# A graph layer's message sums: half-unit padding ahead of odd blocks, and in the last stage selectors on GpSimd, a floor in PSUM, and turning between the sums

## The chip, the cores and the metric

The kernel runs on one core of a Trainium2 chip. The metric is the device time of one execution in microseconds, the median of several runs. The engines are TensorE (PE in the profile, its weight loads PEld), VectorE (DVE), ScalarE (ACT), GpSimd (POOL) and SyncE (SP), which here only issues DMAs.

## The reference

```python
x, src, dst, edge = ...        # (6250, 128), (100000,), (100000,), (100000, 128), float32
h = concatenate([x[src], x[dst], edge]) @ W + b
h = (h - mean(h)) * rsqrt(var(h) + 1e-5) * gamma + beta
msg = relu(h)
out = segment_sum(msg, src, 6250)
return layernorm(x + out)
```

`src` and `dst` are drawn at random; the edges are sorted by `dst`. The sum goes over `src`, which is unsorted.

## The kernel before

Nodes are cut into `NB` = 49 blocks of 128 by `src`, edges into `NG` = 98 groups of 1024 in the order given. The work has three parts.

**Groups.** For each group the edge features are turned and multiplied by the last third of W, the `dst` part is added by a one-hot matmul, and the 1024 rows of 129 numbers (128 values and the node's number in its block) are scattered by GpSimd, eight indirect DMAs a group (L677), to a DRAM buffer `rows`, sorted by the block of `src`. Each block has a region there: its edges in order of arrival, and behind them `UNIT` = 256 rows of padding, whose node number is -1, so that it meets no selector. The start of each region is made from the block counts at the beginning (`room_of`, `end_at`, `start`). SP writes the padding (`fill_pad`, L531), four blocks per group in the first 13 groups, from one SBUF tile `fill`; the last block's padding goes first, since idle places of the list read it.

**Pairs.** The filled regions are read back in units of 256 rows, two units (a pair) at a time. A list made on the chip (`list_rows`, `list_places`, `list_entries`) gives each place the block and the offset of its unit, in the order in which units become full. Four places are given to each group from group 7 on; where too few units are full, a place stays idle and reads padding. A pair `s` goes through these steps, spread over several steps of the loop so that the engines work on different pairs at once:

- SP loads its 512 rows to `hs` (`load_pair`, four steps ahead, when the buffer is free after `pre`, L546).
- VectorE compares node numbers with `iota_row`: `sel`, 128x512, one-hot (`selectors`, L1582), two steps ahead. The four buffers come free with the sums.
- TensorE turns `sel` (`turn_selectors`, L924, one step ahead), ScalarE copies it to `selT` (`copy_selT`, L1169), TensorE picks the `src` part of each row, twelve matmuls (`select_a`, L934).
- VectorE adds the loaded rows to it: `pre` (`add_pair`, L1557). ScalarE sums squares (L1177) and takes the root (L1183), VectorE the reciprocal (L1565).
- VectorE scales and applies the floor, which stands for beta and relu: four operations, 128x128 each (`messages`, L1573), with `floor` in SBUF.
- TensorE sums the messages into blocks with `sel` (`sum_tile`, L910, four tiles of two matmuls), two steps later, and VectorE adds both results to `sums` (`add_run`, L1549), three steps later.

Steps 0 to 173 are written into the groups' loop, two per group. From 174 on they run alone: this is the drain (`drain_trips`), written out to step 179 and then as a loop of trips of four steps, whose number is computed on the chip from the number of full units and idle places (`trips`). `TRIP_ADD` is -304 and the shift 3. In the drain each engine runs its own list in order:

```python
PE:   turn_selectors(s+1); sum_pair(s-2); select_a(s+1)
ACT:  copy_selT(s+1); squares(s); roots(s)
DVE:  add_pair(s); add_run(s-3, 0); root_inverse(s-1); add_run(s-3, 1); messages(s-1); selectors(s+2)
```

The order between engines is by semaphores alone: turning waits for `n_sel`, selecting for ScalarE's copy (`n_selTc`), `pre` for `n_a`, sums for `n_msg`, selectors for `n_o` (the sums that used their buffer) and for the loaded rows. GpSimd has no work in the drain.

**Final rows.** y = sums times gain (GpSimd, L709), plus x and more terms, then the layer norm (VectorE L1775 to L1792, ScalarE) and the output.

## Time and profile before

| | us |
|---|---|
| median of 3 runs | 1763.23 (1761.63 to 1763.72) |
| profiled execution | 1767.91 |
| its span on the core | 1766.0 |
| VectorE, TensorE, ScalarE, GpSimd busy | 960.2, 1214.0, 718.9, 770.3 |

The profile is of one execution. Its page gives the busy time of each engine over the whole span and in slices; the trace behind it can be asked for any stretch. Times in the rows count from the start of the span. The groups end near 1585 us, the drain near 1723.

### The profile page before, as it was taken

The numbers are of one execution on the slowest core, as the hardware profiler recorded it, in microseconds if no ns is written. First come the engines' busy times: TensorE is split into PE (matmuls) and PEld (weight loads), VectorE is DVE, ScalarE is ACT, GpSimd is POOL, SyncE is SP. The second block draws the span as 40 slices with busy tenths as digits, with TensorE's granted clock in tenths as the row PEclk, the third lists the DMA queues.
The fourth block names the chain that finished last, engine by engine and source line by source line (L and its number), as shares of the span: only waits on it lengthen the run. The fifth ranks groups of instructions, "written<-read, shape, count | busy, mean of one in ns | idle before, by whom it ended". The sixth has DMA issues, their size and how long they took to land.

```text
span 1766.0 us, 36601 instructions
## 1 busy us (share of the span) xinstructions
PE 1214.0 (69%) x10009; PEld 1061.0 (60%) x10010; DVE 960.2 (54%) x2822; ACT 718.9 (41%) x2854; POOL 770.3 (44%) x808
## 2 busy tenths in 40 slices
PE   6688766676676766666666666766666766647775
PEld 5555656666566665666666566665656666546662
DVE  7633345555455555445545545554455545439997
ACT  4223333434334443334434434443334433336766
POOL 0334555444454445455444455444555444550003
PEclk9778788778778878788887888787788778869998
DMA  7544444444434444444444444444344434313322
GB/s 213 165 116 130 134 145 146 128 113 120 138 116 129 129 117 116 123 130 130 123 115 122 130 122 129 127 112 131 112 130 128 127 111 119 108 57 91 90 67 73
DMA packets 184266, 214.69 MB, mean 122 GB/s; under 512 B 51478, under 2 KB 133610, under 8 KB 184080
## 3 DMA queue, kind: packets, MB, share of 16 engines
q1 hardware_dynamic: 158044, 159.86, 33.8%
q0 software_dynamic: 25088, 51.83, 8.4%
q8 instruction: 83, 1.36, 0.3%
q10 hardware_dynamic: 948, 0.79, 0.2%
q14 instruction: 103, 0.84, 0.2%
HBM read 145.91 MB, written 66.47 MB: 120 GB/s over the span
## 4 chain that ended last, share of the span: by engine, by line
PE 41%; another core or an unknown queue 22%; issue 18%; ACT 9%; DVE 6%; DMA 2%; DVEq 2%; SPq 0%; ACTq 0%
PE bank L956 11%; PE bank L934 7%; PE bank L910 7%; PE bank L850 5%; ACT late L1177 4%; PE bank L924 3%; PE bank L963 2%; DVE late L1573 2%; ACT turn L1139 2%; PE bank L840 1%; PE bank L838 1%; DVEq L490 1%; DMA tabB<-room 1%; ACT late L1183 1%
## 5 line engine op out<-in xcount | busy, mean ns | idle before, releaser
L677 POOL DMA_INDIRECT rows<-p,pos_idx x784 | 754.3, 962 | 825.4 <-ACT p L1143 537.3
L1139 ACT COPY turn<-bank 128x512 f32<-128x512 f32 x196 | 114.8, 586 | 705.1 <-remote 533.1
L956 PE MATMUL bank<-wc,turn 128*128 128x128 f32 x1552 | 300.8, 354 | 67.4 <-ACT turn L1139 54.7
L934 PE MATMUL bank<-room 128*128 x2640 | 251.8, 250 | 93.7 <-issue 67.2
L956 PEld LDWEIGHTS bank<-wc,turn 128*128 128x128 f32 x1552 | 260.5, 254 | 92.2 <-ACT turn L1139 77.5
L934 PEld LDWEIGHTS bank<-room 128*128 128x128 bf16 x2640 | 208.7, 115 | 115.1 <-issue 104.0
L1177 ACT ACTIVATE late<-room 128x128 f32<-128x128 f32 x880 | 260.7, 302 | 3.0 <-issue 1.5
L1573 DVE SCALAR_TENSOR_TENSOR late<-room,late,floor 128x128 f32<-128x128 f32 x880 | 252.6, 349 | 0.8 <-issue 0.5
L910 PE MATMUL bank<-late 128*128 128x129 f32 x1504 | 233.3, 299 | 25.9 <-issue 23.5
L910 PEld LDWEIGHTS bank<-late 128*128 128x128 f32 x1504 | 211.8, 215 | 18.6 <-issue 18.2
L1169 ACT COPY room<-bank 128x512 bf16<-128x512 bf16 x220 | 129.2, 587 | 210.6 <-remote 111.1
L1557 DVE TENSOR_TENSOR room<-bank,room 128x512 f32<-128x512 f32 x132 | 90.7, 687 | 190.0 <-remote 189.4
L850 PE MATMUL bank<-ident,p 128*128 128x128 f32 x784 | 147.7, 320 | 37.8 <-issue 36.5
L1557 DVE TENSOR_TENSOR room<-bank,late 128x512 f32<-128x512 f32 x88 | 60.4, 687 | 204.1 <-remote 204.0
L1177 ACT ACTIVATION_READ_ACCUMULATOR late<-room 128x1 f32 x880 | 168.2, 191 | 0.0
L840 PE MATMUL bank<-turn,before 128*128 128x50 bf16 x704 | 58.2, 202 | 151.3 <-issue 151.3
L840 PEld LDWEIGHTS bank<-turn,before 128*128 128x128 bf16 x704 | 44.0, 113 | 182.6 <-issue 182.6
L850 PEld LDWEIGHTS bank<-ident,p 128*128 128x128 f32 x784 | 102.1, 167 | 63.4 <-issue 62.8
L1549 DVE TENSOR_TENSOR room<-room,bank 128x129 f32 x440 | 126.2, 287 | 23.6 <-issue 19.3
L924 PE MATMUL bank<-ident_bf,late 128*128 128x128 bf16 x752 | 86.1, 243 | 46.0 <-DVE late L1582 28.6
L1143 ACT COPY p<-bank 128x512 f32<-128x512 f32 x196 | 111.7, 570 | 6.2 <-PE bank L963 3.2
L963 PE MATMUL bank<-win,turn 126*128 126x128 bf16 x784 | 97.6, 261 | 0.0
(237 smaller groups left out, 1255.4 us busy)
## 6 DMA issues: line engine op xcount, KB each, us to landing
p<-in_edge_attr_dram SPq DMA_DIRECT2D x98, 512.0 KB
room<-rows SPq DMA_DIRECT2D x264, 129.0 KB
near_bc<-near SPq DMA_DIRECT2D x98, 256.0 KB
late<-rows SPq DMA_DIRECT2D x176, 129.0 KB
rows<-p,pos_idx POOLq DMA_INDIRECT x784
rows<-fill SPq DMA_DIRECT2D x49, 129.0 KB, 3.2
win<-tabB SPq DMA_DIRECT2D x196, 31.5 KB
tabB<-room SPq DMA_DIRECT2D x12, 384.0 KB, 3.2
```

Source lines behind the costliest of these rows:

```text
L677: nc.gpsimd.indirect_dma_start(rows_ap, bass.IndirectOffsetOnAxis(pos_idx[:, k, j:j + 1], 0), stage[:, k, j, :], None).then_inc(st_free[k] ...
L850: mm = pe.transpose(bank[E_BANK][:, t * P:(t + 1) * P], e_sb[:, k, j * D:(j + 1) * D], ident[:])
L910: mm = pe.matmul(o[:, jj // UJ, :], sel[kk][:, jj, :], msg_room[:, o_at(s, c, -2), jj, :], start=(jj % UJ == 0), stop=(jj % UJ == UJ - 1))
L924: mm = pe.transpose(turned[:, j * P:(j + 1) * P], sel_top[sel_at(s, c, 1, fused)][:, j, :], ident_bf[:])
L934: mm = pe.matmul(bank[A_BANK + b2][:, jj * D:(jj + 1) * D], selT[b2][:, jj * P:(jj + 1) * P], tabA[:, bass.ds(at[jj // UJ], 1), part, :], ...
L956: pe.matmul(bank[H_BANK + h][:, t * D:(t + 1) * D], eT[h][:, t * P:(t + 1) * P], wc[:, 2, :], start=(t == 0), stop=False, skip_group_check ...
L963: mm = pe.matmul(bank[H_BANK + h][:, t * D:(t + 1) * D], pick_t, win[0:WR, k, h, :], start=False, stop=(t == 3), skip_group_check=True)
L1139: nc.scalar.copy(eT[h], bank[E_BANK][:]).then_inc(eT_ready, 1)
L1169: nc.scalar.copy(selT[b2], turned).then_inc(n_selTc, 1)
L1177: a = nc.scalar.activation(junk[b2][:, j, :], pre[b2][:, j, :], ACT.Square, accum_out=ssq[:, b2, j:j + 1])
L1557: nc.vector.tensor_tensor(pre[b2], bank[A_BANK + b2][:].rearrange("p (j d) -> p j d", j=SJ), hs[kk][:, :, 0:D], ALU.add).then_inc(n_pre, 1)
L1573: a = nc.vector.scalar_tensor_tensor(msg_room[:, b2, j, 0:D], pre[b2][:, j, :], rstd[:, b2, j:j + 1], floor[:], ALU.mult, ALU.max)
```

## The change

Four things are changed.

1. Each odd block's region begins with `SHIFT` = 128 rows of padding. `front` holds 0 for even blocks and 128 for odd ones; `base` is the region's start and `start` that of its edges. The list counts units from `base`. The padding of an even block is written together with the next block's front: 384 rows in one DMA. The source tile `fill` is now one row of 129 numbers per partition, repeated, so each DMA's pieces are 516 bytes instead of 1032. Even blocks are written first, and the first load of a pair waits for all 25 of them.
2. In the drain, from step `BY_POOL` = 178 on, GpSimd makes the selectors, with four operations of 128x128 instead of one of 128x512.
3. The floor is copied to PSUM once, in step 177, and the messages from step 178 on read it there.
4. In the drain TensorE turns the selectors of the next pair between the second and the third of the four sum tiles, no longer ahead of them.

```diff
+    SHIFT = UNIT // 2
+        BY_POOL = FUSED + 4
             def fill_pad(bk):
-                at = sp.value_load(pad_i[0:1, bk:bk + 1], min_val=0, max_val=E + NB * UNIT)
-                sp.dma_start(rows_ap[bass.ds(at, UNIT), :].rearrange("(p j) c -> p (j c)", j=UJ),
-                             fill_rows).then_inc(s_fill0 if bk == NB - 1 else s_fill, 16)
+                n = UNIT + SHIFT if bk % 2 == 0 and bk < NB - 1 else UNIT
+                at = sp.value_load(pad_i[0:1, bk:bk + 1], min_val=0, max_val=E + NB * UNIT + NB // 2 * SHIFT)
+                sp.dma_start(rows_ap[bass.ds(at, n), :].rearrange("(p j) c -> p j c", j=n // P),
+                             fill[:].to_broadcast([P, n // P, ROW])).then_inc(s_fill if bk % 2 else s_fill0, 16)
+
+            pads = [bk for bk in range(NB) if bk % 2 == 0] + [bk for bk in range(NB) if bk % 2]
+            EVEN = (NB + 1) // 2
...
-                    if isinstance(g, int) and 1 <= g and 4 * g - 4 < NB - 1:
-                        for bk in range(4 * g - 4, min(4 * g, NB - 1)):
+                    if g >= 1:
+                        for bk in pads[4 * g - 4:4 * g]:
                             fill_pad(bk)
...
                         if s + FETCH == 0:
                             sp.wait_ge(s_list, 1)
-                            sp.wait_ge(s_fill0, 16)
+                            sp.wait_ge(s_fill0, 16 * EVEN)
...
+            nc.gpsimd.memset(front[:, 0:BK:2], 0.0).then_inc(s_iota, 1)
+            nc.gpsimd.memset(front[:, 1:BK:2], float(SHIFT)).then_inc(s_iota, 1)
...
+            def selectors(s, c, q, r):
+                hk = hs_at(s, c, q, r, 2)
+                pool.wait_ge(hs_ready[hk[0]], hk[1] * 32)
+                pool.wait_ge(n_o, s - 1)
+                settle()
+                for j in range(SJ):
+                    a = nc.gpsimd.tensor_scalar(sel[(c + 2) % RING][:, j, :], iota_row[:], hs[hk[0]][:, j, D:ROW], None, ALU.is_equal)
+                a.then_inc(n_sel, 1)
+
+            def step(s, c, q, r, on):
+                if isinstance(s, int) and s < BY_POOL:
+                    return
+                if isinstance(s, int) and s == BY_POOL:
+                    pool.wait_ge(n_sel, BY_POOL + 2)
+                if on(2):
+                    selectors(s, c, q, r)
+            drain_trips(pool, trip_count(pool), step)
...
             def step(s, c, q, r, on):
                 if on(1):
                     at = entry(pe, regs, blk_i, s + 1, NB - 1)
-                    turn_selectors(s, c)
-                if on(-2):
-                    sum_pair(s, c)
+                for jj in range(SJ):
+                    if jj == SJ // 2 and on(1):
+                        turn_selectors(s, c)
+                    if on(-2):
+                        sum_tile(s, c, jj)
                 if on(1):
                     select_a(s, c, at)
...
-            link(nc.vector.tensor_scalar(room_of[:], bank[3][:, 0:BK], float(UNIT), None, ALU.add))
+            link(nc.vector.scalar_tensor_tensor(room_of[:], bank[3][:, 0:BK], float(UNIT), front[:], ALU.add, ALU.add))
             link(nc.vector.tensor_tensor_scan(end_at[:], room_of[:], room_of[:], 0.0, ALU.add, ALU.bypass))
-            nc.vector.tensor_tensor(start[:], end_at[:], room_of[:], ALU.subtract).then_inc(s_base, 1)
+            link(nc.vector.tensor_tensor(base[:], end_at[:], room_of[:], ALU.subtract))
+            nc.vector.tensor_tensor(start[:], base[:], front[:], ALU.add).then_inc(s_base, 1)
...
-                nc.vector.tensor_copy(fl_i[:, 0, :], cum[:])
-                link(nc.vector.tensor_tensor(fl_i[:, 1, :], cum[:], cnt[:], ALU.subtract))
+                link(nc.vector.tensor_tensor(fl_i[:, 0, :], cum[:], front[0:NR, :], ALU.add))
+                link(nc.vector.tensor_tensor(cum[:], cum[:], cnt[:], ALU.subtract))
+                link(nc.vector.tensor_tensor(fl_i[:, 1, :], cum[:], front[0:NR, :], ALU.add))
...
                 if on(-1):
-                    messages(s, c)
-                if on(2):
+                    messages(s, c, floor[:] if isinstance(s, int) and s < BY_POOL else floor_ps)
+                if on(2) and isinstance(s, int) and s < BY_POOL:
                     selectors(s, c, q, r, iota_row[:])
+                if isinstance(s, int) and s == BY_POOL - 1:
+                    dve.wait_ge(st_ready, 2 * NG)
+                    nc.vector.tensor_copy(floor_ps, floor[:]).then_inc(s_floor_ps, 1)
+                    dve.wait_ge(s_floor_ps, 1)
```

## Rows read from the trace of the kernel before

**Rows 1.** The page's busy times by engine, and its group of all messages.

```profile
PE 1214.0 (69%) x10009; PEld 1061.0 (60%) x10010; DVE 960.2 (54%) x2822; ACT 718.9 (41%) x2854; POOL 770.3 (44%) x808
...
L1573 DVE SCALAR_TENSOR_TENSOR late<-room,late,floor 128x128 f32<-128x128 f32 x880 | 252.6, 349 | 0.8 <-issue 0.5
```

**Rows 2.** Stretches: length, busy PE, PEld, DVE, ACT, POOL, clock, DMA share, GB/s.

```profile
500.00:1000.00 500.00, 341.77 (x2912) 310.19 (x2911) 260.24 (x745) 197.39 (x812) 246.15 (x256) 0.81 0.44 124
...
1640.00:1680.00 40.00, 31.09 (x338) 27.43 (x338) 39.23 (x126) 28.79 (x140) 0.00 (x0) 1.00 0.33 93
```

**Rows 3.** Groups by line, 1600 to 1708 us: busy us, mean ns, idle us.

```profile
L1582 DVE TENSOR_TENSOR late<-iota_row,room 128x512 f32<-128x512 f32 x38 | 26.0, 685 | 0.0
L1557 DVE TENSOR_TENSOR room<-bank,room 128x512 f32<-128x512 f32 x37 | 25.4, 686 | 0.0
L1169 ACT COPY room<-bank 128x512 bf16<-128x512 bf16 x37 | 21.7, 586 | 29.8 <-PE bank L924 29.8
...
L924 PE MATMUL bank<-ident_bf,late 128*128 128x128 bf16 x148 | 14.4, 219 | 24.4 <-DVE late L1582 24.4
```

**Rows 4.** Timeline of one drain step: start us, length us, engine, line.

```profile
1656.49 0.69 DVE L1557 TENSOR_TENSOR room<-bank,room 128x512 f32<-128x512 f32 x1
...
1656.71 0.38 PE L924 MATMUL bank<-ident_bf,late 128*128 128x128 bf16 x4 [0.53 <-DVE late L1582]
...
1656.93 1.11 PE L910 MATMUL bank<-late 128*128 128x129 f32 x8
...
1657.13 0.59 ACT L1169 COPY room<-bank 128x512 bf16<-128x512 bf16 x1 [0.67 <-PE bank L924]
...
1657.71 1.14 DVE L1573 SCALAR_TENSOR_TENSOR late<-room,late,floor 128x128 f32<-128x128 f32 x4
...
1657.88 1.03 PE L934 MATMUL bank<-room 128*128 x12
...
1659.37 0.69 DVE L1557 TENSOR_TENSOR room<-bank,room 128x512 f32<-128x512 f32 x1
```

**Rows 5.** Timeline of the last steps of the drain.

```profile
1715.48 1.03 PE L934 MATMUL bank<-room 128*128 x12
...
1716.61 0.69 DVE L1557 TENSOR_TENSOR room<-bank,room 128x512 f32<-128x512 f32 x1
...
1717.85 1.13 DVE L1573 SCALAR_TENSOR_TENSOR late<-room,late,floor 128x128 f32<-128x128 f32 x4
...
1719.11 1.16 PE L910 MATMUL bank<-late 128*128 128x129 f32 x8 [1.34 <-DVE late L1573]
```

**Rows 6.** Timeline around the first steps of the drain.

```profile
1585.91 0.59 ACT L1169 COPY room<-bank 128x512 bf16<-128x512 bf16 x1 [13.64 <-remote]
...
1586.65 1.49 PE L934 MATMUL bank<-room 128*128 x12 [10.45 <-ACT room L1169]
...
1598.41 0.69 DVE L1557 TENSOR_TENSOR room<-bank,room 128x512 f32<-128x512 f32 x1
```

**Rows 7.** A memset of GpSimd's (group), and the timeline in the final rows.

```profile
L651 POOL MEMSET ones_f<- 128x128 f32 x1 | 0.2, 194 | 0.0
...
1723.00 13.26 POOL L709 TENSOR_TENSOR room<-room,gain 128x896 f32<-128x896 f32 x7 [139.93 <-DVE room L1549]
...
1730.13 1.12 DVE L1775 TENSOR_TENSOR room<-room,bank 128x512 f32<-128x512 f32 x2
...
1733.46 0.95 DVE L1788 SCALAR_TENSOR_TENSOR p<-p 128x7 f32<-128x7 f32 x1
...
1744.60 0.17 DVE L1788 SCALAR_TENSOR_TENSOR p<-p 128x7 f32<-128x7 f32 x1
...
1749.92 1.15 DVE L1775 TENSOR_TENSOR room<-room,bank 128x512 f32<-128x512 f32 x2
```

**Rows 8.** Padding writes: ns on SP's queue, and the page's size and landing.

```profile
L531 SPq DMA_DIRECT2D rows<-fill x49: 3/333/1156, 70.7 to 248.2; - x49
...
rows<-fill SPq DMA_DIRECT2D x49, 129.0 KB, 3.2
```

More of the change, by code:

```diff
@@ L52, in bass_gnn_resnorm @@
     IDLE = -(4 * FIRST_FULL - 4 - NB * (UNIT - 1) // UNIT)
-    MOST = E // UNIT + IDLE
+    SHIFT = UNIT // 2
+    MOST = (E + NB // 2 * SHIFT) // UNIT + IDLE
     PAIRS = 4
@@ L69, in bass_gnn_resnorm @@
     near = nc.dram_tensor("near", (NG, GE), BF16)
-    rows = nc.dram_tensor("rows", (E + BK * UNIT + 2 * GE, ROW), F32)
+    rows = nc.dram_tensor("rows", (E + BK * UNIT + NB // 2 * SHIFT + 2 * GE, ROW), F32)
     rows_ap = rows.ap()
@@ L135, in bass_gnn_resnorm @@
         end_at = sb("end_at", [P, BK])
+        front = sb("front", [P, BK])
+        base = sb("base", [P, BK])
         start = sb("start", [P, BK])
@@ L144, in bass_gnn_resnorm @@
         blk_i, off_i = pair_i[:, :, 0:2], pair_i[:, :, 2:4]
-        fill = sb("fill", [P, UJ, ROW])
+        fill = sb("fill", [P, 1, ROW])
         x_in = sb("x_in", [P, NB, D])
@@ L275, in bass_gnn_resnorm @@
         turned = bank[T_BANK][:].bitcast(BF16)[:, 0:SJ * P]
+        floor_ps = bank[3][:, 0:D]
         iota_ps = bank[T_BANK][:, 256:256 + P]
@@ L323, in bass_gnn_resnorm @@
         s_pads = sem("pads_known")
-        s_fill = sem("pads_filled")
+        s_fill = sem("odd_pads_filled")
         s_l0 = sem("units_by_group_known")
@@ L328, in bass_gnn_resnorm @@
         s_lb = sem("unit_of_each_place_spread")
-        s_fill0 = sem("last_pad_filled")
+        s_fill0 = sem("even_pads_filled")
         s_l1 = sem("list_rows_made")
@@ L342, in bass_gnn_resnorm @@
         s_iota_ps = sem("iota_in_psum")
+        s_floor_ps = sem("floor_in_psum")
         s_rbase = sem("rank_bases_made")
@@ L525, in _ @@
             sp.wait_ge(s_near_st, 16)
-            fill_rows = fill[:].rearrange("p j c -> p (j c)")
             def fill_pad(bk):
-                at = sp.value_load(pad_i[0:1, bk:bk + 1], min_val=0, max_val=E + NB * UNIT)
-                sp.dma_start(rows_ap[bass.ds(at, UNIT), :].rearrange("(p j) c -> p (j c)", j=UJ),
-                             fill_rows).then_inc(s_fill0 if bk == NB - 1 else s_fill, 16)
+                n = UNIT + SHIFT if bk % 2 == 0 and bk < NB - 1 else UNIT
[4 more added lines that the diff above has]
+            EVEN = (NB + 1) // 2
             regs = [sp.alloc_register(f"sp_off{v}") for v in range(2)]
@@ L576, in step @@
                         load_near(g + AHEAD, kk)
-                    if isinstance(g, int) and g == 1:
+                    if g == 1:
                         sp.wait_ge(s_pads, 1)
-                        fill_pad(NB - 1)
-                    if isinstance(g, int) and 1 <= g and 4 * g - 4 < NB - 1:
-                        for bk in range(4 * g - 4, min(4 * g, NB - 1)):
+                    if g >= 1:
+                        for bk in pads[4 * g - 4:4 * g]:
                             fill_pad(bk)
@@ L609, in _ @@
                 sp.wait_ge(s_list, 1)
-                sp.wait_ge(s_fill0, 16)
+                sp.wait_ge(s_fill0, 16 * EVEN)
                 for k in range(RING):
@@ L617, in _ @@
                 pair_trips(sp, step)
-            sp.wait_ge(s_fill, 16 * (NB - 1))
+            sp.wait_ge(s_fill, 16 * (NB - EVEN))
             def step(s, c, q, r, on):
@@ L714, in _ @@
             pe.wait_ge(s_const, 1)
-            pe.wait_ge(s_iota, 10)
+            pe.wait_ge(s_iota, 12)
             def turn_indices(v, banks):
@@ L1266, in link @@
                 dve.wait_ge(s_dve, chain[0])
[L1268 removed]
+            dve.wait_ge(s_iota, 12)
             nc.vector.tensor_scalar(ident[:], iota_row[:], iota_col[:], None, ALU.is_equal).then_inc(s_const, 1)
@@ L1463, in list_rows @@
                 link(nc.vector.tensor_tensor(f_now, fl_i[:, 1, 0:NB], put[:, 0:NB], ALU.subtract))
-                nc.vector.scalar_tensor_tensor(put[:, NB:2 * NB], f_now, float(UNIT), start[0:NR, 0:NB], ALU.mult, ALU.add)
-                link(nc.vector.tensor_tensor(cum[:], cum[:], cnt[:], ALU.subtract))
+                nc.vector.scalar_tensor_tensor(put[:, NB:2 * NB], f_now, float(UNIT), base[0:NR, 0:NB], ALU.mult, ALU.add)
                 nc.vector.tensor_tensor(cum[:], cum[:], start[0:NR, :], ALU.add).then_inc(s_rbase, 1)
@@ L1565, in root_inverse, with messages @@
                 nc.vector.reciprocal(rstd[:, b2, :], std[:, b2, :]).then_inc(n_rs, 1)
-            def messages(s, c):
+            def messages(s, c, least=floor[:]):
                 b2 = (c - 1) % 2
@@ L1573, in messages @@
                     a = nc.vector.scalar_tensor_tensor(msg_room[:, b2, j, 0:D], pre[b2][:, j, :], rstd[:, b2, j:j + 1],
-                                                       floor[:], ALU.mult, ALU.max)
+                                                       least, ALU.mult, ALU.max)
                 a.then_inc(n_msg, 1)
```

3 lines of the change are left out of this document (1 added, 2 removed).

## The prediction

> **What bounds the kernel now.** I read the page first, then the busy time by stretch, then groups, timeline and waits of the last stage. The page gives no engine above 69% [rows 1], so no engine's total decides; the stages must be read apart. Up to about 1585 us the edge groups and the summing of pairs run together, with VectorE half busy and the DMA engines at 0.44 [rows 2]; the diff touches this stage only through the padding writes. The next stage, the drain, has VectorE busy 39.2 of 40 us [rows 2], with nothing idle in front of its large operations [rows 3], while TensorE waits 24.4 us and ScalarE 29.8 us over 37 steps, TensorE for VectorE's selectors, ScalarE for TensorE's turned ones [rows 3]. So VectorE sets the drain's step, 1656.49 to 1659.37, 2.88 us [rows 4]: its work costs 0.60 each for the selectors and for the sum `pre` (start to next start), about 1.05 for four messages and 0.6 for the two run sums and the reciprocal. Then, from about 1723 to 1766, the final rows follow, in which the change does nothing.
>
> **Removed: steps.** The diff changes the list of units, and this can be worked out from the reference's `src`. Today every block's count is cut in units of 256: 367 full ones and 49 partial ones. All blocks fill at nearly the same rate, so in the early groups fewer than four units per group are full, and the list holds 18 idle places. With 128 rows ahead of the 24 odd blocks, these fill half a unit earlier: 379 full ones, but no idle place. The trip formula gives (367 + 18 - 304) >> 3 = 10 before and (379 + 0 - 304) >> 3 = 9 after. Before makes 180 + 4 x 10 = 220 steps, which agrees with 880 messages of four per step [rows 1]; after makes 216. The four steps all come off the drain.
>
> **Removed: selectors on VectorE.** From step 178 on GpSimd makes them. VectorE's work per step falls to 2.88 - 0.60 = 2.28 us. Whether the step falls as far is set by who is late next. Four loops have to be worked out.
>
> *TensorE with ScalarE's copy.* The new order is half the sums, turn, half the sums, select. Before, four sum tiles (0.95, 1656.93 to 1657.88) lay between turning and selecting and hid the copy of the turned selectors; now two do. Half the sums take 0.48; from the first turn to the start of ScalarE's copy are 0.42, the copy takes 0.59 [rows 4], the hand-over back to TensorE 0.15 (a copy from 1585.91 to 1586.50, selecting at 1586.65) [rows 6], selecting 1.03, 0.9 of it before the next weights go in (my estimate: the last result follows the last start by 0.1 to 0.2). Sum 2.54 us per step. ScalarE alone is busy 28.8 of 40 us [rows 2], 2.07 of a step.
>
> *Messages to messages.* Messages of a step end, 0.13 to the start of the sums [rows 5], 0.48 half the sums, 0.42 + 0.59 + 0.15 turn and copy, 1.03 selecting, 0.10 to VectorE's `pre` (1716.51 to 1716.61) [rows 5], and from `pre` to the end of the messages 2.36 (1656.49 to 1658.85) [rows 4]. Sum 5.26 us, and it spans two steps: 2.63 us per step. With the old order the sums would cost 0.95 here, but turning and copy would be out of the chain: 4.57, or 2.29 per step. So the new order costs this loop something, while it serves the next.
>
> *GpSimd.* A selector buffer comes free with the sums of the same step, and its result is turned in the next step. From the start of turning: 0.22 to the second half of the sums, 0.48, some 0.16 to its last result (sums end at 1658.04, selecting starts at 1657.88) [rows 4], 0.13 hand-over, T for GpSimd, 0.13 back: 1.12 + T. T is not in the trace. From below: a 128x128 memset takes 0.19. From above: seven two-input operations of 128x896 take 13.26 [rows 7], 1.89 each or 2.1 ns per element, so 0.27 for 128 elements, plus as much as 0.14, about one hand-over, for an operation's own time. Four of 0.19 to 0.41, and some 0.2 for waits and the turn count: T = 1.0 to 1.8. One input rather than two lies nearer the memset; I take 0.28 each, T = 1.3, and this loop needs 2.42. It becomes the bound only above T = 1.5. The Trainium skill (GPSIMD Engine Reference, Elementwise — side-by-side cycle accounting) gives 1.8 cycles per element for a tight one-input loop; at 1.2 GHz that is an estimate of 0.19 us for 128 elements without dispatch, and by it the sum would be the same.
>
> *Loads.* A pair's rows are asked for after `pre`, four steps ahead. A padding write of the same 129 KB landed 3.2 us after its issue [rows 8]. `pre` 0.69, two issues 0.7, landing 3.2, T 1.3, 0.13 hand-over and 2.3 from turning to the next `pre` are 8.3 us over four steps, 2.1 per step. No bound, at a DMA share of 0.33 now [rows 2].
>
> So the step should be 2.63 us, by the messages' loop. TensorE's granted clock is 1.00, the 2.4 GHz level, through the drain [rows 2], and its terms above are at that level; it idles less after than before (0.65 of 2.88 us [rows 3, 4]; then 2.63 less its 2.2 of work), so I expect no fall. The floor in PSUM costs nothing either way: operations of 512 elements take 685 ns with both inputs in SBUF and 686 with one in PSUM [rows 3].
>
> **Sum.** Before, from `pre` of step 178 at 1598.41 [rows 6] to that of the last step, 219, at 1716.61 [rows 5], are 118.2 us in 41 intervals. After, the last step is 215: 37 x 2.63 = 97.3, and 0.4 for the copy of the floor (0.69 for 512 elements is its bound from above [rows 3]; it has 128, and a wait). Gain 20.5 us, of which the four steps are 11.5 at the old step and the shorter step 37 x 0.25 = 9.3. Everything behind the last step is unchanged.
>
> **Added in front.** VectorE gets two linked small operations (block starts, list rows) at about 0.2 each; GpSimd's two memsets take under 0.2 each [rows 7] and lie beside the first loads. The 49 padding writes remain 49 issues on SP's queue at 0.33 us [rows 8], in groups 1 to 13, but move 128 descriptors of 1032 bytes to 256 or 384 of 516, and 6.5 to 8.1 MB. Behind them on the queue are edges, windows and pair loads, loaded three groups ahead. The pair loads of group 9 now wait for 25 writes instead of one; all are issued by group 7, so two groups hide it. Extra bytes at the 124 GB/s of [rows 2] are 13 us of transfers over 13 groups with engines half idle. Bounds 0 and 6 us; I take 1, and 0.5 for VectorE's chain.
>
> Total: 20.5 - 1.5 = 19.0 us. The profiled execution took 1767.9 (span 1766.0), so 1748.9 for one like it; the median of the runs lies 4.7 lower, 1763.2, and gives **1744 us**.
>
> **Rivals.**
>
> *Loops shorter than my sums, VectorE the bound.* Hand-overs add up to a third of the sum and may overlap. At VectorE's 2.28: 37 x 2.28 = 84.4, gain 33.4 - 1.5, 1731 us. For it: VectorE now runs without any gap. Against: each term of the messages' loop is a row, and they follow on one another by the code's own waits. Values from 2.28 to 2.5: 0.14.
>
> *GpSimd the bound.* T above 1.5, up to 2.0: steps of 2.64 to 3.12. At T = 1.8, 2.92: 108.0, gain 9.8 - 1.5, 1755 us. For it: a loop in software, with a scalar read per partition, of which the trace has no row. Chance 0.22.
>
> *Slower: GpSimd and VectorE block one another.* In the final rows, while GpSimd multiplies (to 1736.3), VectorE's 128x7 operation with two SBUF inputs took 0.95 against 0.17 later [rows 7]. The Trainium skill (SBUF — State Buffer, SBUF: two separate sides) calls the shared port pair an exclusive lock, held for the whole instruction, against VectorE operations with two SBUF inputs or in a two-port mode; by that rule, the trace agrees. In the drain `pre` and run sums have one input in PSUM, and two such operations took 1.12 beside GpSimd and 1.15 after it [rows 7]; the messages would have two in SBUF but for the moved floor. Should the messages (whose scalar is in SBUF too) still be held for each GpSimd operation, a step has 2.28 + 4 x 0.3 = 3.5 us: 129.5 + 0.4 + 1.5 against 118.2, 1776 us. It decides from a step of 3.14 us on (37 x 3.14 + 1.9 = 118.1), which GpSimd alone reaches at T = 2.0, 0.45 per operation. Both ways together 0.08.
>
> *The list does not shrink.* It follows from the inputs by integers. If a trip were kept, four steps of 2.63 return: 1755 us. 0.02.
>
> **Numbers.** The forecast (step 2.5 to 2.64, 1739 to 1745, some more with costlier writes, to 1748) has 0.5; shorter loops 0.14; GpSimd as the bound 0.22; blocking 0.08; the rest, 0.06, lies in the list and in writes that cost over 4 us. Faster or slower by less than 0.2%, 3.5 us, is about what a measurement of this kernel can't tell from no change. The range goes from VectorE's bound, 1731, to T = 1.8 with 1 us over, 1756. Faster 0.89, same 0.03, slower 0.08.
>
> **What would show it.** 864 messages; pre's distance in the drain near 2.63 with gaps of some 0.3 us before it on VectorE, released by TensorE's selecting; TensorE waiting 0.3 for ScalarE's copy; GpSimd's four operations within 1.5 us. Gaps before turning, released by GpSimd, would mean T is the bound; messages longer than 1.05 the blocking. I would be wrong above all in T, and in the first stage: should its 1500 us shift by 0.3% with the longer program or the padding, that is as much as a quarter of the gain.

## The result, and the profile after

The changed kernel took 1780.25 us (median of 4 runs, 1778.23 to 1782.45) against 1763.16 for the kernel before (4 runs): a ratio of 1.008, interval 1.0059 to 1.0101. I had forecast 1744 us, 1731 to 1756. It is slower by 17 us, and outside the range.

The profiled execution took 1781.42 us, its span is 1779.6. From the page, two groups (count, busy us, mean ns, idle us and what ended it):

```profile
L1207 ACT ACTIVATE late<-room 128x128 f32<-128x128 f32 x864 | 256.3, 302 | 4.5 <-DVE room L1588 2.5
...
L722 POOL TENSOR_SCALAR late<-iota_row,room 128x128 f32<-128x128 f32 x144 | 84.4, 603 | 59.4 <-PE bank L938 49.0
```

The first row is ScalarE's squares, four per step as the messages are: 864 in place of 880 [rows 1], so the list shrank to 216 steps as worked out. Of the second, the new row, look at the mean: GpSimd's operation takes 603 ns. I had put 0.28 us there.

The stretches that [rows 2] showed, now:

```profile
500.00:1000.00 500.00, 341.40 (x2904) 309.22 (x2904) 259.43 (x740) 197.41 (x810) 246.99 (x256) 0.80 0.44 123
1640.00:1680.00 40.00, 29.23 (x271) 22.47 (x269) 25.67 (x89) 23.35 (x115) 26.67 (x46) 1.00 0.28 73
```

The first stage is as it was. In the drain VectorE went from 39.2 busy to 25.7 of 40 us, and the number of matmuls from 338 to 271: every engine but GpSimd does less per microsecond, at the same granted clock of 1.00. Groups of 1600 to 1708 us, as in [rows 3]:

```profile
L722 POOL TENSOR_SCALAR late<-iota_row,room 128x128 f32<-128x128 f32 x123 | 72.1, 603 | 53.5 <-PE bank L938 44.3 <-issue 9.2
L938 PE MATMUL bank<-late 128*128 128x129 f32 x240 | 41.1, 293 | 18.8 <-issue 17.7 <-DVE room L1580 1.1
...
L1604 DVE SCALAR_TENSOR_TENSOR late<-room,late,bank 128x128 f32<-128x128 f32 x124 | 34.6, 343 | 0.2 <-issue 0.2
...
L1588 DVE TENSOR_TENSOR room<-bank,room 128x512 f32<-128x512 f32 x31 | 21.5, 693 | 35.8 <-PE bank L962 35.7
```

VectorE now waits 35.7 us for TensorE's selecting, over 31 steps. TensorE idles 18.8 us ahead of the sums, and the release given is "issue": it waited for no other engine. The chain of waits through one step and into the next (start us, us, what):

```profile
1656.34 0.60 ACT room L1199
1656.94 0.14 issue
1657.08 1.06 PE bank L962 x12
1658.14 0.51 issue
1658.65 0.71 PE bank L938 x4
...
1659.84 0.60 ACT room L1199
...
1661.63 0.93 issue
1662.56 0.71 PE bank L938 x4
```

From copy to copy are 3.50 us, 0.51 of them a gap between selecting and the sums that my sum did not have; where a trip of four steps ends the gap is 0.93. The timeline of the same step for GpSimd, with the messages and the turning beside it:

```profile
1657.01 2.34 POOL L722 TENSOR_SCALAR late<-iota_row,room 128x128 f32<-128x128 f32 x4 [1.16 <-PE bank L938]
...
1659.40 0.23 PEld L952 LDWEIGHTS bank<-ident_bf,late 128*128 128x128 bf16 x4 [0.23 <-POOL late L722]
...
1659.42 1.12 DVE L1604 SCALAR_TENSOR_TENSOR late<-room,late,bank 128x128 f32<-128x128 f32 x4
```

GpSimd's four operations take 2.34 us, not 1.3, and the next four start at 1660.51, again 3.50 later. Its loop and TensorE's are nearly equal: the weight load of the turning stands idle for 0.23 us ahead of GpSimd's last result, but the chain of TensorE above is held by it for no more than 0.05. Where the time went: the first `pre` of the changed part, step 178, starts at 1598.91 (1598.41 before, [rows 6]), the last at

```profile
1729.17 0.69 DVE L1588 TENSOR_TENSOR room<-bank,room 128x512 f32<-128x512 f32 x1 [1.31 <-PE bank L962]
```

130.3 us for 37 intervals, 3.52 each, where I had 97.7. What lies ahead cost 0.5 us (forecast 1.5), what lies behind 50.4 instead of 49.4 us.

### The profile page after: what moved, and what is told of

Its sections match the earlier page's. It is cut to its first block and busy times, and to the rows that moved or that the text cites. A ratio compares the mean times of both kernels' runs of the same rounds, so it can differ in the third digit from the quotient of the medians.

```text
span 1779.6 us, 36364 instructions
## 1 busy us (share of the span) xinstructions
PE 1214.2 (68%) x9913; PEld 1049.1 (59%) x9914; DVE 930.6 (52%) x2752; ACT 712.2 (40%) x2814; POOL 857.1 (48%) x954
## 5 line engine op out<-in xcount | busy, mean ns | idle before, releaser
L962 PE MATMUL bank<-room 128*128 x2592 | 244.1, 248 | 102.6 <-issue 66.1
L962 PEld LDWEIGHTS bank<-room 128*128 128x128 bf16 x2592 | 201.9, 114 | 130.1 <-issue 120.5
L1207 ACT ACTIVATE late<-room 128x128 f32<-128x128 f32 x864 | 256.3, 302 | 4.5 <-DVE room L1588 2.5
L1604 DVE SCALAR_TENSOR_TENSOR late<-room,late,floor 128x128 f32<-128x128 f32 x708 | 203.8, 349 | 0.4 <-issue 0.3
L722 POOL TENSOR_SCALAR late<-iota_row,room 128x128 f32<-128x128 f32 x144 | 84.4, 603 | 59.4 <-PE bank L938 49.0
L866 PE MATMUL bank<-cum,ident 98*128 98x50 f32 x176 | 39.6, 254 | 87.8 <-issue 87.5
```

The source lines that it names most:

```text
L962: mm = pe.matmul(bank[A_BANK + b2][:, jj * D:(jj + 1) * D], selT[b2][:, jj * P:(jj + 1) * P], tabA[:, bass.ds(at[jj // UJ], 1), part, :], ...
L1207: a = nc.scalar.activation(junk[b2][:, j, :], pre[b2][:, j, :], ACT.Square, accum_out=ssq[:, b2, j:j + 1])
L1604: a = nc.vector.scalar_tensor_tensor(msg_room[:, b2, j, 0:D], pre[b2][:, j, :], rstd[:, b2, j:j + 1], least, ALU.mult, ALU.max)
```

## The experiments

Both originals and the six kernels down to the shared selectors in the table ran where the groups are much faster: the kernel before has a median of 1250.42 to 1252.18 us there. Its drain is the same, 2.87 us a step, so the drain's numbers carry over, and each ratio is against the kernel before measured beside it. The nine below ran where it takes 1762 to 1766, as in the first result. The expectations speak of two chips, but chips 3 and 7 stand in the record for runs of both kinds, so it isn't shown that the chip makes the difference. Below, "fast groups" and "slow groups" stand for the two kinds. "Step" is the mean distance of `pre` from step 182 to the last one.

| kernel | us | ratio (interval) | step |
|---|---|---|---|
| as before | 1250.42 | 1 | 2.87 |
| as changed | 1270.82 | 1.016 (1.0131 to 1.0189) | 3.54 |
| list alone | 1248.3 | 0.9973 (0.9955 to 0.999) | 2.88 |
| selectors back on VectorE | 1263.46 | 1.0096 (1.007 to 1.0122) | 3.39 |
| floor back in SBUF | 1274.51 | 1.0168 (1.0137 to 1.0199) | 3.55 |
| GpSimd on half the columns | 1268.07 | 1.0124 (1.009 to 1.0157) | 3.39 |
| VectorE's selectors, one load a trip | 1260.12 | 1.0083 (1.0061 to 1.0106) | 3.32 |
| selectors shared, old order | 1265.64 | 1.0117 (1.0089 to 1.0144) | 3.43 |
| changed, old order | 1803.87 | 1.0243 (1.0223 to 1.0264) | 4.22 |
| before, new padding writes | 1765.55 | 1.0014 (1.0 to 1.0027) | 2.87 |
| list, one load a trip | 1760.94 | 0.9992 (0.9979 to 1.0006) | 3.08 |
| changed, constant for the scalar | 1778.46 (one run) | | 3.40 |
| list alone, again | 1757.31 | 0.9953 (0.9937 to 0.9969) | 2.87 |
| list and new order | 1777.29 | 1.0056 (1.0036 to 1.0076) | 3.40 |
| before, even padding first | 1766.34 | 0.9997 (0.9985 to 1.001) | 2.87 |
| list, pieces of 1032 bytes | 1753.18 | 0.9937 (0.9916 to 0.9959) | 2.87 |
| list alone, third time | 1753.61 | 0.9941 (0.9919 to 0.9962) | 2.87 |

**Both kernels again.**

> The kernel before, for a trace on the chip of the experiments: steps of 2.88 us in the drain from step 182 to 219, 42 or so of them, as in the first trace. If the list's gain of 11.5 us is eaten in front by the padding writes, group 10 starts here up to 8 us earlier than with the new padding; if not, it starts at the same time within 2 us.

> The changed kernel, on the chip of the experiments: steps of 3.55 us as in its first trace, set by the loop through GpSimd (1.16 us and four operations in 2.34 us), so 13 us more than the list alone less what it shares with it: a ratio to before of 1.008 at a time of 1763 us, 1.015 where the groups run faster.

With fast groups the change loses 20 us, 3 more than in the first result. The steps are those of the first result, so the drain's loss does not hang on how fast the groups are. Group 10's first scatter starts at 187.3 us in the kernel before and at 187.7 in the changed one, so up to there the padding writes delay nothing.

**The parts one by one.** The list alone: VectorE makes all selectors, the floor stays in SBUF, TensorE keeps its order.

```diff
-                for jj in range(SJ):
-                    if jj == SJ // 2 and on(1):
-                        turn_selectors(s, c)
-                    if on(-2):
-                        sum_tile(s, c, jj)
+                if on(1):
+                    turn_selectors(s, c)
+                if on(-2):
+                    sum_pair(s, c)
...
-                if on(2) and isinstance(s, int) and s < BY_POOL:
+                if on(2):
                     selectors(s, c, q, r, iota_row[:])
```

> Only part 1 of the change: the 128 rows ahead of odd blocks, their padding writes and the list. Selectors on VectorE, floor in SBUF, turning ahead of all sums, as before. Theory (the loss of the whole change is GpSimd's selectors; the list is a gain): 216 steps of 2.88 us, so four steps or 11.5 us less than before, and nothing lost in front: 1752 us. Rival (the padding writes cost in the groups): the drain is 11.5 us shorter, but starts some us later, and the time stays within 3 us of 1763.

It is 3.9 us faster than the kernel before; the four steps are gone and the step's length is the old one. Why not 11.5 us is taken up below.

The changed kernel with only the selectors back on VectorE (GpSimd's loop deleted, and the last change above):

> The changed kernel with the selectors of the drain back on VectorE; the list, the floor in PSUM and the turning between the sums stay. Theory: VectorE bounds the step again at 2.88 us, the loop from messages to messages (2.63 by my sum) lies below it, so 1752 us like the list alone. Rival (the new order of TensorE or the floor in PSUM has part in the loss): a step above 2.95 us, gaps ahead of VectorE's pre released by TensorE's selecting, 1756 us or more.

3.39 us a step, with GpSimd doing nothing in the drain: the rival was right. So TensorE's new order, or the floor in PSUM, costs 0.5 a step; a later run leaves only the order. Here is the chain from the sums to the end of selecting, and the piece between selecting and the next sums, again "issue":

```profile
1134.58 0.71 PE bank L921 x4
1135.29 0.24 PE bank L935 x4
1135.53 0.02 issue
1135.55 0.59 ACT room L1182
1136.14 0.15 issue
1136.29 1.05 PE bank L945 x12
1137.34 0.54 issue
1137.88 0.71 PE bank L921 x4
```

The gap is 0.51 to 0.54 us, and 0.93 where a trip's branch lies in it. One ordinary step is 0.51 + 0.71 + 0.24 + 0.02 + 0.59 + 0.15 + 1.05 = 3.27 us, one with the branch 0.4 more. What TensorE's queue does in the gap is seen by asking for the line that reads the list (`entry`, ns minimum/median/maximum), here, in the step shown, and in the kernel before:

```profile
L497 PEldq TENSOR_LOAD <-pair_i x29: 533/537/539, 1102.8 to 1197.9; - x29
```

```profile
L497 PEldq TENSOR_LOAD <-pair_i x1: 533/533/533, 1137.1 to 1137.1; - x1
```

```profile
L490 PEldq TENSOR_LOAD <-pair_i x18: 532/537/545, 1650.4 to 1699.2; - x18
```

A load of four registers from SBUF, 0.54 us each step, in both kernels. In the step shown it runs from 1137.09 to 1137.63, from just before the last selecting matmul ends to 0.25 us before the sums; register instructions fill that rest. So load and gap are not the same stretch, though equally long, and what the load costs has to be shown by taking it out. Before, the queue came to it ahead of the turning, and it lay in TensorE's wait for the selectors (24.4 us over 37 steps, 0.66 each [rows 3]).

The floor back in SBUF:

```diff
-                    messages(s, c, floor[:] if isinstance(s, int) and s < BY_POOL else floor_ps)
+                    messages(s, c)
...
-                if isinstance(s, int) and s == BY_POOL - 1:
...
```

> The changed kernel with the messages reading the floor in SBUF throughout; GpSimd makes the selectors. Theory (each GpSimd operation takes 0.58 us by itself and is slowed by nobody): if the two engines do not block one another, step 3.5 us and 1780 us as the changed kernel. Rival (blocking): a message with two SBUF inputs waits for GpSimd's operation or the other way round: four messages take well over 1.05 us, GpSimd's four operations over 2.34 us, step 3.8 us or more, 1790 us or more.

The step stays (3.55; messages 346 ns). It says little of the blocking:

```profile
1150.50 2.35 POOL L722 TENSOR_SCALAR late<-iota_row,room 128x128 f32<-128x128 f32 x4 [1.15 <-issue]
...
1152.90 1.13 DVE L1604 SCALAR_TENSOR_TENSOR late<-room,late,floor 128x128 f32<-128x128 f32 x4
1154.01 1.18 POOL L722 TENSOR_SCALAR late<-iota_row,room 128x128 f32<-128x128 f32 x2 [1.16 <-PE bank L938]
```

The messages run from 1152.90 to 1154.03, nearly all in the gap in which GpSimd waits. Twice a message that started first lies beside a longer part of an operation of GpSimd's, 0.19 and 0.22 us of it; the operation takes 662 and 692 ns there, the message 347 and 343. The second of them:

```profile
L722 POOL TENSOR_SCALAR late<-iota_row,room x1: 692/692/692, 1221.4 to 1221.4; 128x128 f32<-128x128 f32 x1
```

In the changed kernel, with the floor in PSUM, the same kind of overlap (0.26 us, operations from 1603.78 and 1607.28) leaves 603 and 602 ns. So messages with all inputs in SBUF do hold GpSimd up, a little and seldom; a message that starts inside an operation of GpSimd's, but for its last 0.03 us, is in no run with the floor in SBUF.

GpSimd on 64 of 128 columns (half of each selector is not made):

```diff
-  a = nc.gpsimd.tensor_scalar(sel[(c + 2) % RING][:, j, :], iota_row[:], ...
+  a = nc.gpsimd.tensor_scalar(sel[(c + 2) % RING][:, j, 0:P // 2], iota_row[:, 0:P // 2], ...
```

> The changed kernel with GpSimd's four operations on 64 of the 128 columns each: half of each selector isn't made, so sums of half the nodes are left wrong from step 180 on; all else runs as in the changed kernel. Theory 1 (the time is per element): each operation takes 0.3 us, T is 1.2 us, the loop through GpSimd needs 2.4 us, and the loop from messages to messages bounds the step at 2.63 us: 1747 us. Theory 2 (mostly fixed time per operation): 0.5 us each, T 2.0 us, step 3.2 us, 1768 us.

```profile
L722 POOL TENSOR_SCALAR late<-iota_row,room 128x64 f32<-128x64 f32 x144 | 60.5, 443 | 60.1 <-PE bank L938 45.3
```

443 against 603 ns: by a straight line through these two, 2.5 ns per element and 0.28 us of fixed time, so each theory held in part. GpSimd's loop is 0.64 us shorter, the step only 0.15, and stops at 3.39, where TensorE's loop stands. So GpSimd's loop sets the last 0.15 us of the step, and TensorE's stands right under it.

**What the fixed time is.** The changed kernel with a constant in place of the node number (the drain's selectors are wrong by it):

```diff
-  ..., iota_row[:], hs[hk[0]][:, j, D:ROW], None, ALU.is_equal)
+  ..., iota_row[:], float(j), None, ALU.is_equal)
```

> The changed kernel, but each of GpSimd's four operations in the drain compares with a constant instead of with the node number of its partition, so the selectors of the drain are wrong. It asks what the 0.28 us of fixed time in an operation of 0.60 us is. Theory: it is the operation's own start, and 128 columns at 2.5 ns each do not depend on where the number comes from: 580 to 610 ns, steps of 3.5. Rival: reading the scalar of each partition is a good part of it: under 500 ns, and steps of 3.4, TensorE's loop.

```profile
L722 POOL TENSOR_SCALAR late<-iota_row 128x128 f32<-128x128 f32 x144 | 72.3, 529 | 65.7 <-PE bank L938 54.3
```

529 ns: the scalar per partition costs 74 ns of 603. The time lies between the two that I had named, but the step is 3.40, TensorE's loop once more.

**The order.** The list alone with TensorE's new order:

> The list alone and TensorE's new order; selectors on VectorE, floor in SBUF. Theory: TensorE's own load of the block numbers, which the old order hides in its wait for the selectors, makes the step 3.39 us as in the experiment with the floor in PSUM, since the floor matters to neither loop: 19 us slower than the list alone, ratio 1.004 to 1.008. Rival: the floor in PSUM had a part in that step, and this one is 3.2 us or less, or 3.6 or more.

3.40 us, as with the floor in PSUM: the order alone is what lengthens TensorE's loop. Against the list alone measured beside it it loses 20 us, for 37 steps of 0.53. The other way round, the changed kernel with the old order (the first nine lines of the list's diff and nothing else):

> The changed kernel with TensorE's old order (turn, four sum tiles, select); GpSimd still makes the selectors, the floor is in PSUM. Theory: with GpSimd's four operations at 2.34 us the order decides how much of TensorE's sums lies in GpSimd's loop. With the new order two sum tiles lie ahead of the moment at which the selector's buffer is free, with the old order all four do: turn 0.23, sums 1.11, hand-over 0.20, GpSimd 2.34, back 0.06, that is 3.94 us per step in place of 3.54, or 15 us more than the changed kernel over 37 steps, a ratio of 1.026 to 1.030 against the kernel before on this chip. Rival: the order makes no difference (3.5 us per step, 1.016), since GpSimd's loop and TensorE's own loop hide in one another. Second rival: the new order is itself a loss (it costs TensorE's own loop), and this is faster than the changed kernel: under 1.014.

An undisturbed step is 3.95 us, as expected (3.94):

```profile
1649.88 2.33 POOL L722 TENSOR_SCALAR late<-iota_row,room 128x128 f32<-128x128 f32 x4 [1.61 <-PE bank L938]
...
1652.51 1.12 PE L938 MATMUL bank<-late 128*128 128x129 f32 x8
...
1653.83 2.33 POOL L722 TENSOR_SCALAR late<-iota_row,room 128x128 f32<-128x128 f32 x4 [1.61 <-PE bank L938]
...
1656.62 2.04 PE L938 MATMUL bank<-late 128*128 128x129 f32 x8
```

The mean is 4.22, since TensorE, which now waits 1.7 us in each step, does not keep the 2.4 GHz level: eight sums take 2.04 in place of 1.12 us in some steps, and the granted clock of a stretch is 0.76 to 0.93. One of 20 us (the clock stands behind the busy times):

```profile
1640.00:1660.00 20.00, 13.86 (x119) 12.31 (x116) 9.63 (x35) 10.28 (x50) 10.48 (x18) 0.76 0.24 66
```

The fall of the clock was in none of my theories. The ratio, 1.0243, missed the 1.026 to 1.030 that I had written: the 15 us that I expected would have given about 1.017. With GpSimd's selectors the new order is worth 26 us (37 steps of 4.22 against 3.52), some 16 of them by the undisturbed step of 3.95; with VectorE's it costs 20.

**TensorE's load taken out.** Selectors on VectorE, new order, and the block numbers of four steps loaded at the first of them:

```diff
-                    at = entry(pe, regs, blk_i, s + 1, NB - 1)
+                    if isinstance(s, int):
+                        at = entry(pe, regs, blk_i, s + 1, NB - 1)
+                    else:
+                        if c == 0:
+                            pe.load(regs4, pair_i[0:1, bass.ds(s + 1, PAIRS), :].rearrange("o s v -> o (s v)"))
...
+                        at = held[0][2 * c:2 * c + 2]
```

> Selectors on VectorE, turning between the sums, and TensorE's register loads of the list's entries made once per trip of four steps instead of once per step. Theory (the new order exposes the register load of 0.54 us between selecting and the sums, which the wait for selectors hid before): three of four gaps of 0.5 to 0.9 us go, the step falls from 3.39 to 2.9 us, 16 us less than with the load in each step. Rival (the chain of sums, turning, copy and selecting is itself too long, or the gap has another cause): the step stays above 3.2 us.

```profile
1125.04 0.68 DVE L1580 TENSOR_TENSOR room<-bank,room 128x512 f32<-128x512 f32 x1
1127.90 0.69 DVE L1580 TENSOR_TENSOR room<-bank,room 128x512 f32<-128x512 f32 x1
1132.86 0.69 DVE L1580 TENSOR_TENSOR room<-bank,room 128x512 f32<-128x512 f32 x1 [0.52 <-PE bank L945]
```

Three of four steps are nearly all 2.85 to 2.88, VectorE's bound: without the load the new order costs nothing. This fits the sum, 3.27 - 0.51 = 2.76, below 2.88. The fourth step takes 4.0 to 5.0, more than the load was worth: its load of 16 registers takes 1.1 us, the branch lies in it, and four sums after the gap take 1.10 us in place of 0.71. So the mean, 3.32, lies where I had put the rival, though the mechanism was the theory's. The same edit on the list alone:

> The list alone, with TensorE's load of the block numbers in the drain made once per trip of four steps instead of in each. Theory: with selectors on VectorE and the old order TensorE waits 0.65 us a step for VectorE behind its load of 0.54 us, so the load is hidden and leaving it out of three steps in four gains nothing there: 2.88 us per step; the fourth step, whose load takes 1.1 us and has the branch, may take up to 0.4 us more. Ratio 0.997 to 1.001 against the kernel before. Rival: the load is exposed in every order, and steps without it fall below 2.8 us: under 0.995.

```profile
1645.78 0.68 DVE L1579 TENSOR_TENSOR room<-bank,room 128x512 f32<-128x512 f32 x1
1649.31 0.69 DVE L1579 TENSOR_TENSOR room<-bank,room 128x512 f32<-128x512 f32 x1 [0.19 <-PE bank L945]
1652.20 0.68 DVE L1579 TENSOR_TENSOR room<-bank,room 128x512 f32<-128x512 f32 x1
```

Steps without the load stay at 2.88, so in the old order it was hidden; the fourth takes 3.5 us, in two cases 4.3 or more. This settles the cause from the other side, and one load a trip is no gain over the list alone in either order.

**An attempt at a better split.** Old order, floor in SBUF, load once per trip; GpSimd makes two of the four tiles, VectorE the other two in one operation of 128x256.

```diff
-                for j in range(SJ):
+                for j in range(SJ // 2):
                     a = nc.gpsimd.tensor_scalar(sel[(c + 2) % RING][:, j, :], ...
-                a.then_inc(n_sel, 1)
+                a.then_inc(n_half, 1)
...
+                        pe.wait_ge(n_half, s - BY_POOL)
...
+                    lo = 0 if isinstance(s, int) and s < BY_POOL else SJ // 2
...
+                    nc.vector.tensor_tensor(sel[kk][:, lo:SJ, :], iota_row ...
```

> The new list; turning ahead of all sums as before; the floor in SBUF; from step 178 on GpSimd makes two of the four selector tiles and VectorE the other two; TensorE's register loads once per trip. Theory: VectorE needs 2.28 + 0.33 = 2.61 us, TensorE about 2.5, the loop through GpSimd 0.22 + 1.11 + 0.20 + 1.17 + 0.06 = 2.76 us: a step of 2.76, 4 to 5 us less than the list alone. Rival (blocking: two-input messages now run beside GpSimd's operations): four messages take 1.4 us or more, GpSimd's operations over 0.62 us each, the step is 2.9 us or more and the kernel no faster than the list alone.

```profile
1132.37 0.42 DVE L1810 TENSOR_TENSOR late<-iota_row,room 128x256 f32<-128x256 f32 x1
1132.38 1.46 POOL L723 TENSOR_SCALAR late<-iota_row,room 128x128 f32<-128x128 f32 x2 [1.78 <-PE bank L939]
...
1134.08 0.38 PE L953 MATMUL bank<-ident_bf,late 128*128 128x128 bf16 x4 [1.01 <-POOL late L723]
...
1135.61 1.37 POOL L723 TENSOR_SCALAR late<-iota_row,room 128x128 f32<-128x128 f32 x2 [1.77 <-PE bank L939]
```

Missed, 3.43 us: in these steps TensorE waits 1.0 for GpSimd's half, which takes 1.37 to 1.46 where two operations of the changed kernel take 1.18, and GpSimd waits 1.77 for the sums and not 1.59. The durations of one (ns minimum/median/maximum), here and in the changed kernel:

```profile
L723 POOL TENSOR_SCALAR late<-iota_row,room x52: 593/662/885, 1111.5 to 1198.3; 128x128 f32<-128x128 f32 x52
```

```profile
L722 POOL TENSOR_SCALAR late<-iota_row,room x136: 594/603/622, 1600.3 to 1719.0; 128x128 f32<-128x128 f32 x136
```

The first of the two operations, beside VectorE's compare, takes 727 to 885 ns; the second, mostly beside `pre`, 593 to 597. In most steps the compare starts first. In two GpSimd starts 0.26 us ahead of it, as here at 1129.30:

```profile
1129.55 0.51 DVE L1810 TENSOR_TENSOR late<-iota_row,room 128x256 f32<-128x256 f32 x1
```

GpSimd's operation lasts from 1129.30 to 1130.02, and the compare takes 0.51 in place of 0.42 us.

**Where the rest of the list's gain is.** The kernel before with the new padding writes (all the lines below), then with the new order of them and the wait for 25 alone (all but the change of the pieces in the second line):

```diff
-  sp.dma_start(... "(p j) c -> p (j c)" ..., fill_rows).then_inc(s_fill0 if bk == NB - 1 else s_fill, 16)
+  sp.dma_start(... "(p j) c -> p j c" ..., fill[:].to_broadcast([P, UJ, ROW])).then_inc(s_fill if bk % 2 else s_fill0, 16)
+  pads = [bk for bk in range(NB) if bk % 2 == 0] + [bk for bk in range(NB) if bk % 2]
-  sp.wait_ge(s_fill0, 16)
+  sp.wait_ge(s_fill0, 16 * EVEN)
```

> The kernel before with the new form of the padding writes alone: source of one row repeated (pieces of 516 bytes instead of 1032), even blocks first, and the first pair load waits for 25 writes instead of one. The list and its 220 steps stay, 256 rows for each block. Theory: the padding writes are what takes 7 us of the 11.5 that the shorter list should give, by holding up groups 10 to 13: a ratio of 1.003 to 1.006, and group 13 starts 2 us or more later. Rival: they cost nothing (0.999 to 1.002), and the missing time of the list alone lies in the extra rows ahead of the odd blocks, or in how one execution of the groups differs from another.

> The kernel before with the even blocks' padding written first and the first pair load behind 25 writes, but with the old pieces of 1032 bytes. The new form as a whole cost 3 us (ratio 1.0014). Theory: the pieces of 516 bytes cost it, since the writes are all out by group 7, two groups ahead of the wait: 0.9995 to 1.0005 here. Rival: the wait for 25 writes costs it: 1.001 to 1.002.

3 us (0 to 5) with the small pieces, nothing without, though the two intervals overlap. The list alone twice more, and once with pieces of 1032 bytes (384 rows from 96 partitions; three small tiles are shrunk or share storage to make room):

```diff
-  fill = sb("fill", [P, 1, ROW])
+  fill = sb("fill", [P, UJ, ROW])
-  ... "(p j) c -> p j c", j=n // P), fill[:].to_broadcast([P, n // P, ROW]))
+  ... "(p i j) c -> p i (j c)", i=pieces, j=UJ), fill[0:parts] ... .to_broadcast([parts, pieces, UJ * ROW]))
```

> The list and the padding alone, the same kernel as in the experiment of that name, which gave 3.9 us on a chip whose groups take 10.2 us. If this chip is like the one of the first result (groups of 15.5 us): four steps of 2.88 less are 11.5 us, the new form of the writes alone costs 2.5 (0 to 5), so 7 to 10 us faster, 0.9945 to 0.996. Rival: the rows ahead of the odd blocks cost as much again here, and the gain is 4 us or less, 0.9975 or more.

> The list alone, with padding written in pieces of 1032 bytes as before (384 rows from 96 partitions, twice two rows each). Theory: the small pieces cost the 2 to 3 us that the list alone lacks, so this one gains them: 11 us faster than the kernel before on a chip whose groups take 15.5 us, ratio 0.993 to 0.995, and 2 to 3 us faster than the list alone of the same call. Rival: the pieces do not matter, 0.995 to 0.9965, as the list alone.

> The list alone a third time, for comparison on the same chip: 0.995 to 0.9965 where groups take 15.5 us, 0.9955 to 0.999 where they take 10.2.

With slow groups the list alone gains 8.5 and 8.8 us of its 11.5. The ratio of the large pieces, 0.9937, lies in the theory's range, but the list alone measured beside it has 0.9941, a difference of 0.4 us and not 2 to 3: the pieces make no difference that is seen, and the theory of small pieces falls. With fast groups, where the list alone gained 3.9, the DMA share of the stretch with the padding rises to full (first the kernel before, then the list alone):

```profile
60.00:240.00 180.00, 158.57 (x1276) 121.86 (x1277) 106.11 (x284) 81.15 (x240) 116.02 (x120) 0.88 0.67 186
```

```profile
60.00:240.00 180.00, 155.40 (x1275) 119.78 (x1275) 105.35 (x285) 81.65 (x242) 114.14 (x120) 0.89 1.02 193
```

and with slow groups only from 0.47 to 0.52 and 0.58 in two traces of the list alone. The traces also show where the loss lies: with fast groups, from group 10's first scatter to group 13's are 31.9 us in the kernel before (one trace) and 34.6 to 37.4 in seven traces of kernels with the new list; with slow groups 46.5 against 47.3 and 47.5. That the writes cost more where the DMA engines are full fits this; it was not tested, and what takes the last 3 us with slow groups stays open.

## Why the prediction was wrong

*The steps removed* held: 216, and the list alone gained 8.5 us of 11.5 with slow groups.

*TensorE with ScalarE's copy*, 2.54 us, is the first step that failed. It summed only the instructions that the timeline shows, half the sums, turning, the copy, selecting. TensorE's own register load, 0.54 us per step, is not counted as busy and lay before in its wait of 0.66. The new order has TensorE wait for the copy inside each step and so uses up that slack; the load comes into the loop. Of the 0.73 us from 2.54 to 3.27, the gap is 0.51, selecting 0.15 (1.05 for 0.9) and half the sums with the turning 0.07. With the branch of each fourth step the measured mean is 3.39, by itself 0.5 us above the old step. It was shown by adding the order alone (3.40), and by taking the load out (2.87). The load was in the trace before as well: TensorE waited 0.66 of 2.88 us, and I had read all of that as free.

*GpSimd*, 1.12 + T with T = 1.3 and a bound of 1.8, is the second: four operations take 2.34. The fixed part of the loop was right, 3.50 - 2.34 = 1.16. The nearest rows were no bound: the memset reads nothing, and the 13.26 us of [rows 7] hides an operation's fixed time in 896 elements, 2.1 ns each, with 0.14 allowed for it; here it is 0.28 and 2.5 ns. The rival "GpSimd the bound" had the right mechanism and a range that ended at 2.0. The Trainium skill (GPSIMD Engine Reference, Elementwise — side-by-side cycle accounting) has 1.8 cycles per element; the estimate of 0.19 us from it is without dispatch, and the row of 603 ns is three times that.

*Messages to messages*, 2.63, from which the forecast came, was never the bound; that it is 2.63 no run shows, only that it is no more than the 2.87 of the steps without the load. *The loads* weren't the bound either: `pre` waited for TensorE's selecting.

*Blocking.* The 1776 us which that rival gave was near, but by luck: the messages took 343 ns each, 349 before [rows 1], and the step was lengthened by other loops. The changed kernel has its floor in PSUM and can't show what the messages would meet in SBUF; where they have it there, it was GpSimd's operation that grew, to 662 and 692 ns, and not the message. The shared split shows more: GpSimd's operation beside VectorE's 128x256 compare, which has both inputs in SBUF, takes 727 to 885 ns. The Trainium skill (SBUF — State Buffer, SBUF: two separate sides) says that of two such operations the one that starts first holds the shared port pair for the whole instruction and the other waits. VectorE starts first, or at the same time, in all but two of the steps, and there the rows agree. Where GpSimd started 0.26 ahead they don't: the compare ended 0.04 after GpSimd's operation, 0.51 long, so it can't have waited for the whole of it.

*The floor* was free, as forecast. *In front* it was 0.5, forecast 1.5. *Behind* it was 1.0 more than forecast, by chance:

```profile
1733.32 2.08 PE L938 MATMUL bank<-late 128*128 128x129 f32 x8 [0.51 <-DVE late L1604]
```

The last eight sums take 2.08 us, 1.16 in the kernel before, and the granted clock from 1733 to 1735.5 is 0.53, near the 1.2 GHz level. The same kernel with fast groups takes 1.16 there at 1.00, and 49.5 us behind its last `pre`.

The sum, set right: 1748.9 + 32.6 (37 steps of 3.52 for 2.63) - 1.0 + 1.0 = 1781.5, measured 1781.4. The two errors don't add: TensorE's alone makes the step 3.39 to 3.40 (measured), GpSimd's alone 3.50 (by its sum; no run has it alone). Put together from the runs, the 17 us of loss are 8.5 gained by the list, 20 lost by the order, and 5.6 lost by GpSimd (37 steps of 3.54 for 3.39). I gave "slower" 0.08 because I had three loops that looked worked out from rows, though one held an unmeasured operation and one an engine whose queue I had not read.

## What to carry to other kernels

Before you take away what an engine waits for, read what its queue does in that wait: register loads and branches are in no busy time and come out as "issue" when the cover goes. An operation that no trace shows is bounded by one of its own kind and size only; a row with ten times the elements hides the fixed time. Work moved to a slower, idle engine must fit the loop that it closes, not the idle time: GpSimd was free for 2.88 us a step, but only 2.88 - 1.16 = 1.7 of them lay between the buffer that it waits for and the turning that waits for it.

## What the runs showed of the hardware

- The same kernel took 1762 to 1766 us in some runs and 1250 to 1252 in others, and chips 3 and 7 gave both. The drain and the final rows are equal; the groups start 15.5 us apart in the one case and 10.2 in the other, though one of GpSimd's scatters lasts 962 and 975 ns (256 and 391 of them in 500 to 1000 us, idle 251 and 119 us). From 500 to 1000 us, for the kernel before with fast groups, to be set beside [rows 2]:

```profile
500.00:1000.00 500.00, 405.03 (x4387) 365.15 (x4386) 382.21 (x1124) 296.73 (x1224) 381.03 (x391) 0.98 0.71 189
```

  Granted clock 0.98 against 0.81, DMA share 0.71 against 0.44. Why is open. Only stages that are alike in both cases can be compared, and ratios only with the kernel before measured beside.
- TensorE's register load: 0.54 us for four registers, 1.1 for sixteen; the latter, once per four steps, made that step 0.6 us longer in the old order.
- TensorE waiting 1.7 us in steps of 3.95 was granted 0.76 to 0.93 of its clock; with gaps of 0.51 to 0.93 in steps of 3.5 it kept 1.00.
- GpSimd's compare of 128x128 with a scalar per partition takes 603 ns, with a constant 529, of 128x64 443.
